# Sums of squares copied out of PSUM by VectorE instead of ScalarE, and TensorE's loop begun at program slot 226 instead of 208

## The reference, cut to what matters

```
for i in range(DEPTH):                                   # DEPTH = 6
    x = attn_layer(shift_tokens(x), Wqkv[i], q_scale[i], k_scale[i], Wo[i]) + x
    x = ffn_layer(shift_tokens(x), ln_g[i], ln_b[i], W1[i], b1[i], W2[i], b2[i]) + x

def attn_layer(x, Wqkv, qs, ksc, Wo):                    # 16 heads of 64
    q, k, v = jnp.split(x @ Wqkv, 3, -1)                 # then split into heads
    q = l2norm(q) * qs                                   # t / max(norm(t), 1e-12)
    k = l2norm(k) * ksc
    q = q * cos * scale + rotate_half(q) * sin * scale
    k = k * cos * inv + rotate_half(k) * sin * inv
    out = local_attention(q, k, v)                       # windows of 32, each sees itself and the one before
    return out.transpose(0, 2, 1, 3).reshape(b, n, INNER) @ Wo
```

## Time and profile before

| | us |
|---|---|
| median of three runs | 4722.76 |
| lowest and highest run | 4708.98 and 4727.22 |
| the profiled execution | 4691.7 |
| its span | 4689.9 |
| TensorE (PE) busy | 3973.2, 85% |
| VectorE (DVE) busy | 3168.6, 68% |
| ScalarE (ACT) busy | 3110.2, 66% |

### The profile page before, as it was taken

One profiled execution on the slowest core, in us unless ns is written; L12 is line 12 of the kernel. 1 busy time (PEld: TensorE's weight loads), 2 busy tenths in 40 slices (PEclk: granted clock), 3 DMA queues, 4 the chain that ended last, 5 costly groups with the idle time before them and its releaser, 6 DMA issues. The chain is left out here.

```text
span 4689.9 us, 172910 instructions
## 1 busy us (share of the span) xinstructions
PE 3973.2 (85%) x68188; PEld 2844.2 (61%) x68188; DVE 3168.6 (68%) x6779; ACT 3110.2 (66%) x8351; POOL 867.3 (18%) x1240
## 2 busy tenths in 40 slices
PE   7968888888888888888888888888888888885678
PEld 4746666666666666666666666666666666663334
DVE  4856776666667666666767666666766676665665
ACT  4836776777777677777767777776777777672233
POOL 0012122122121212112122112121211212110122
PEclk9979999999999999999999999999999999996689
DMA  0034344444334444334444434434444443430000
GB/s 28 1 80 83 75 83 83 87 88 85 77 77 80 96 88 83 79 74 83 92 88 80 82 78 86 92 78 81 83 83 91 82 81 77 80 74 17 3 5 12
DMA packets 126144, 336.58 MB, mean 72 GB/s; under 512 B 32592, under 2 KB 33744, under 8 KB 125264
## 3 DMA queue, kind: packets, MB, share of 16 engines
q0 software_dynamic: 61440, 201.38, 23.6%
q1 hardware_dynamic: 64080, 125.25, 10.6%
HBM read 22.41 MB, written 2.10 MB: 5 GB/s over the span
## 5 line engine op out<-in xcount | busy, mean ns | idle before, releaser
L1173 ACT ACTIVATE loc_probs<-loc_pair,loc_ebias,loc_rnorm 128x64 f32<-128x64 f32 x3072 | 1201.2, 434 | 9.7 <-DVE loc_ebias L1333 7.3
L919 PE MATMUL loc_pair<-loc_hs,loc_wqk 128*128 128x256 f32 x3072 | 748.9, 387 | 27.7 <-issue 19.5
L1173 ACT ACTIVATION_READ_ACCUMULATOR loc_probs<-loc_pair,loc_ebias,loc_rnorm 128x1 f32 x3072 | 723.9, 236 | 0.0
L919 PEld LDWEIGHTS loc_pair<-loc_hs,loc_wqk 128*128 128x128 f32 x3072 | 567.3, 192 | 128.4 <-issue 42.6
L1331 DVE TENSOR_REDUCE loc_mx<-loc_pair 128x8 f32<-128x512 f32 x384 | 264.8, 689 | 469.5 <-PE loc_pair L965 466.6
L868 POOL DMA_DIRECT2D loc_ks<-loc_msin x384 | 331.5, 1008 | 1230.2 <-DVE loc_msin L1281 1193.8
L1155 ACT ACTIVATE loc_sq<-loc_pair 128x1024 f32<-128x1024 f32 x384 | 397.2, 1034 | 211.5 <-PE loc_pair L919 211.5
L868 POOL DMA_DIRECT2D loc_qr<-loc_msin x384 | 332.1, 1006 | 1079.1 <-DVE loc_msin L1281 1061.4
L1281 DVE SCALAR_TENSOR_TENSOR loc_msin<-loc_pair,loc_scal,loc_tab 128x1024 f32<-128x1024 f32 x384 | 490.1, 1276 | 2.1 <-DMA loc_ks<-loc_msin 2.1
L965 PE MATMUL loc_pair<-loc_kr,loc_qr 64*32 64x64 f32 x24576 | 311.0, 226 | 121.8 <-issue 121.8
L965 PEld LDWEIGHTS loc_pair<-loc_kr,loc_qr 64*32 64x32 f32 x24576 | 263.3, 106 | 220.2 <-issue 219.9
(11 more groups left out here) (232 smaller groups left out, 7271.8 us busy)
## 6 DMA issues: line engine op xcount, KB each, us to landing
loc_ks<-loc_msin POOLq DMA_DIRECT2D x384, 256.0 KB, 4.5
loc_qr<-loc_msin POOLq DMA_DIRECT2D x384, 256.0 KB, 5.1
loc_veven<-loc_vodd SPq DMA_DIRECT2D x768, 64.0 KB, 3.5
loc_veven<-loc_vodd SPq DMA_DIRECT2D x384, 128.0 KB, 3.9
loc_wqk<-wqk_dram SPq DMA_DIRECT2D x12, 512.0 KB, 4.2
loc_wv<-wv_dram SPq DMA_DIRECT2D x6, 512.0 KB, 5.9
loc_wo<-wo_dram SPq DMA_DIRECT2D x6, 512.0 KB, 3.5
x<-xT_dram SPq DMA_DIRECT2D x1, 2048.0 KB, 7.4
```

The lines of the kernel that those rows point to most:

```text
L919: ins = nc.tensor.matmul(pairs[b][:, p // 2, (p % 2) * UNIT:(p % 2 + 1) * UNIT], wqk[:, k, w:w + P], hs[u.odd][:, :], start=True, stop=True)
L1173: ins = nc.scalar.activation(probs[x][:, p, hp, :], pairs[b][:, hp, p * 2 * WIN:(p + 1) * 2 * WIN], ACT.Exp, bias=ebias[x][:, k:k + 1], sc ...
```

## The change

The copy of the sums of squares leaves ScalarE's order and enters VectorE's, ahead of `reciprocals(0)`, which itself moves ahead of `norms_in`. The wait that ScalarE had for its own buffer (`nT_ps` of the unit before) is dropped: VectorE has already waited for it in the `norms_in` of the unit before. TensorE's own order is untouched; its loop is asked to begin at slot 226. Lines after 735 move by up to 8, so the copy is line 1281 in the kernel after.

```
@@ -732,7 +732,7 @@
             with nc.Fori(FILL // 2, TOTAL // 2, engines=bass.OrderedEngineSet([eng.engine]), hint_back_edge=True,
-                         head_slot={eng.engine: 208} if eng is nc.tensor else None) as i:
+                         head_slot={eng.engine: 226} if eng is nc.tensor else None) as i:
@@ ScalarE @@
-            def norms_out(u, b):
-                if u is None:
-                    return
-                after(act, norm_ps, u.n)
-                after(act, nT_ps, u.n - 1)
-                nc.scalar.activation(nT[:, :], bank(b)[:, 0:UNIT], ACT.Copy).then_inc(nT_ready, 1)
...
                 values_out(1, at(3), 0)
-                norms_out(at(2), 4)
                 exponentials(1, 0, at(3), 2)
@@ VectorE @@
+            def norms_out(u, b):
+                if u is None:
+                    return
+                after(dve, norm_ps, u.n)
+                nc.vector.tensor_copy(nT[:, :], bank(b)[:, 0:UNIT]).then_inc(nT_ready, 1)
...
                 rotate_sin(3, at(2), 1)
+                norms_out(at(2), 4)
+                reciprocals(0, at(3))
                 norms_in(at(2), 4)
-                reciprocals(0, at(3))
                 newton(at(2))
```

## The result

The changed kernel takes 4787.98 us (median of 4 runs, 4764.51 to 4803.84) against 4719.11 us for the kernel before on the same chip: ratio 1.0143, 95% interval 1.0091 to 1.0195. It is 69 us slower. The forecast was slower by 134 us, 4857 us; the sign and the places are right, the size is about twice too large.

The account below looks back on a forecast made before the run. TensorE's order, with stalls for late 256-slot instruction blocks, was taken as the bound. Slot costs less the copy's 1.8 us gave plus 3.1 us a turn, times 45, minus 5: plus 134 us, 4857 us; overall range 4665 to 4935 us.

Parts of the forecast that it names:

- The copy: Moving the copy from ScalarE to VectorE was to shorten the turn by 1.8 us, bounds 0 and 2.8.
- the whole wait should go: TensorE's wait before L946 for ScalarE's exponentials, 0.90 us twice a turn, was to vanish, as ScalarE goes on 1.40 us sooner.
- part 1: The copy's move to VectorE, minus 1.8 us a turn; wrong if L946 still waits for ScalarE or L938 for VectorE.
- The loop's end: At the closing branch, now in a 13th block, the head's late fetch costs plus 3.3 us a turn, bounds 2.5 and 3.6.
- The clock: TensorE's granted clock falls in more turns after the longer pause at the head: plus 0.8 us a turn, bounds 0 and 1.7.
- Border near the head: The block border comes 30 instead of 48 slots after the loop's head: plus 0.1 us a turn.
- The next: The following border moves ahead of L1064, which then hides no fetch: plus 1.3 us a turn, bounds 0.3 and 1.6.
- The three fast runs further on: Borders in first L965, L1002 and second L965: minus 0.1, 0 and minus 0.5 us a turn, together minus 0.6.
- Rival 2: Fetches start earlier with the borders, closing the three gaps in L965, L1002, L965: minus 4.4 us a turn, 4686 us; chance 0.08.
- Rival 1: At the loop's end the hint fetches the branch's target beside the 13th block: minus 1.0 us a turn, 4673 us; chance 0.20.
- Rival 3: The loop head's place in the block has no effect, only the copy's move counts: 86 us less, 4637 us; chance 0.05.
- Rival 4: The copy's move gives nothing, as VectorE comes late and L938 waits instead: plus 220 us, 4943 us; chance 0.07.

## Why the prediction was right, and where its size was wrong

**That TensorE's order and its instruction blocks set the time: right.** The eight head positions that ran with the copy moved differ by up to 170 us with the same work. Only "nearly all the span" was too much said: 45 turns of 82 us are 3.7 of 4.7 ms.

**The copy: right.** Forecast 1.8 us a turn and 86 us; measured alone 1.76 us a turn and 79 to 100 us. VectorE's copy took 419 ns in that kernel (forecast from L1370's 408) and nothing waits for it: L1288's wait for L938 went from 1.00 us to 0.51 us in the turn shown, as the copy fills the rest. Only "the whole wait should go" fails once the head is at 226, where 23.9 of 66.0 us stay. By the prediction's own sign, "part 1 is wrong if L946 still waits for ScalarE", part 1 fails there in part: behind the slot the copy shortens the turn of the traces by 0.60 us (85.30 to 84.71), not by 1.8.

**The loop's end: right in mechanism, too small.** The 13th block, 633 packets (forecast 636) and a branch far over 3 us are there. The step is 4.0 to 4.4 us longer, not 3.3 and above my upper bound of 3.6. That bound came from the exit, where 1.10 us of L919 still ran and the missing block was the next in order. Here the branch's target comes behind the 13th block, and not because the queue is still busy with it: at 219 that block's fetch has ended 1.42 us before the branch starts, and the head's begins 1.76 us behind the branch's start (medians). From 160 to 218 with the hint it begins 0.6 to 1.1 us before it; at 0 and 52, in 12 blocks, 2.12 and 1.49 us behind it, though the fetch before has long ended there too. In all these kernels it begins 3.5 us or more, at the median, after the start of the fetch before it. What holds it back was not found.

**The clock: right in kind, wrong in size and in what it is worth.** In the loop the clock falls 57 times instead of 21 and stands at the low level for 321 us instead of 72. L919 at the head loses 1.7 us to it. But while it runs slowly the next block arrives, so the gap behind it shrinks by 1.2 us (218 against 219, above). The kernel without the hint, head at 219, separates the clock from the pause, as it has both kinds of turns behind a pause. In 18 of them L919 takes 1.92 us, as at 218: L1002 takes 2.27 us (2.93 at 218) and L1064 3.08. In the other 25 L919 takes 3.03 us, but L1002 1.88 and L1064 2.27. The slow clock costs 1.11 us there and gives 1.20 back at once: up to the end of L978 both kinds take 9.5 to 9.6 us. So a slow clock costs next to nothing where a late block stands right behind it. With the head at 0, where no border follows for 256 slots, the same comparison (11 turns and 32) gives 7.1 and 8.7 us: nothing comes back.

**The borders behind the head: this is the step that failed.** It stood as "Border near the head: plus 0.1" and "The next: plus 1.3 us". I priced each as if the loop's end ran as before. By itself the second was well sized: from 208 to 218, still without a bad end, L1064 and L978 grew by 0.90 and 0.43, 1.33 us. Behind the new pause it was not there to be paid:

| term of the slot, us a turn | forecast | slot alone against before |
|---|---|---|
| loop's end and clock | 3.3 + 0.8 | +3.98 +1.72 |
| border near the head (L1002, L1037) | +0.1 | -1.18 +0.81 |
| next (L1064) | +1.3 | -0.48 |
| first L965 | -0.1 | -0.93 |
| L1002 | 0 | -0.60 |
| second L965 | -0.5 | -0.51 |
| last L946, border of the 13th block | not listed | +0.73 |
| turn | 4.9 | +3.39 |

Small steps not listed make the remaining -0.15 us. The two borders behind the head were forecast at +1.4 us together and came out at -0.85, the largest miss, 2.2 us a turn, some 100 us in 45 turns. What the runs showed in its place: behind the pause the next fetch starts earlier beside the work, and the work in front of it runs slower, so the gaps shrink, even where no border has moved (head 219 without the hint).

**The three fast runs further on: a second miss, of 1.4 us.** They were forecast at -0.6 and gave -2.04. The border in the first L965 moved from inside the run to its front (1.52 us for 128 matmuls instead of 2.46). That this comes with the place and not with the pause is shown by 218 against 219: there the pause comes without a move, and the first L965 changed by -0.15 us and the second L1002 by +0.14. Rival 2 had named this; of the 4.4 us that my bounds allowed the three I had taken 0.6. The other way went the border in the last L946, which I had counted but not priced (+0.73), and the end and its clock (+1.6).

**What this makes of the 134 us.** By the two profiled executions the turn grew by 2.79 us where 3.1 was forecast, and the whole by 112 us. That these lie so close is luck: in the traces the slot costs 1.5 us a turn less than forecast, and the copy behind it gains 1.2 us less (0.60 instead of 1.8). By the medians it is 69 us. The other 43 us of the difference to the profiles are the spread between executions: I added a sum made within one execution, which was a quick one of its kernel, to the median of others. By the medians the slot alone is 135.5 us instead of 220, and the copy behind it 66 instead of 86: the loss was put 85 us too high, and the gain 20. One figure in the working of the range is a slip: with the highs named there the turn grows by 4.8 us, not 4.9, and 4.8 is what gives the top of about 4935 us.

**The rivals.** Rival 1 (target fetched beside the 13th block) is out: the branch lasts 4.7 us. Rival 3 (place without effect) is out: 150 us from one slot; nor is the crossing of a border "mostly hidden", as the Trainium skill has it (Runtime: NRT & Kernel Launch, Instruction fetch mechanics). The same section says that a taken branch whose target isn't in the window forces a fetch before execution goes on. The traces agree: the branch lasts 3.9 us at the median without the hint at 208, and 4.7 us in the kernel after. Rival 4 is out: the copy alone makes 2.0%. Rival 2 (gaps close when the borders move) was half there: 2.0 us a turn of its 4.4. The closing at the head and at L1064 comes with the pause.

## What to carry to other kernels

When a loop's body is fetched anew each turn, count its instruction slots from the head: what stands between the last block border and the closing branch must be long enough to cover the fetch of the head (here 197 slots and more were, 37 and 89 were not). Don't sum stalls that wait for the same chain of fetches: a pause gives the fetches behind it time, and of 6.1 us at a loop's end 2.8 came back in the steps right behind it. Try the parts of a change apart even when their sum looks like noise or a loss: here a 2% gain was bundled with a 3% loss.

## What the runs showed of the hardware that was not expected

- A single instruction slot moved the time by 150 us (4637.28 to 4787.49 us), 3.3 us in each of 45 turns.
- The branch at the loop's end lasted 4.1 to 4.7 us at the median when 0, 7, 37 or 89 slots stood between the last border and the branch (heads 219, 226, 0, 52), and 1.6 to 1.9 us with 197 to 255 (160, 192, 208, 218).
- The hint of the back edge replaces the fetch of the block in order: 591 packets with it, 634 without it, at the same head (208). It is worth 68 to 82 us there, and nothing that can be measured with 7 slots of room in front of the branch (226).
- The fetch of the head starts 0.6 to 1.1 us before the branch when 197 slots or more stand in front of it, and 1.5 to 2.4 us behind the branch's start when 0 to 89 do, with the hint in both cases.
- In the turns shown L919 took 3.42 us behind 4.32 us without work and 3.77 us behind 4.85 us, there at a granted clock of 0.50, instead of 1.99. Behind 3.01 us without work, in the kernel without the hint (head 219), it took 1.99 us in the turn looked at; its step there is 2.57 us on average.
